# Feed-forward part and output projection of a sequence placed one step later from the first gate product on, in a six-layer windowed-attention network

## Chip, core and metric

The kernel runs on one core of one Trainium2 chip. The metric is the device time in microseconds (us) of one launch of the whole program, the median of three runs. The core has five engines that run beside each other and meet at semaphores: PE (TensorE, matmul), DVE (VectorE), ACT (ScalarE), POOL (GpSimd) and SP (SyncE, which issues the DMAs here). Each engine takes its instructions strictly in the order in which they are written: an instruction that waits holds up everything behind it on its engine.

## The reference, cut to what matters

The program computes two outer levels; nearly 70% of its time goes to a network of six layers on 8 sequences of 512 tokens with 128 features. This is the part that the change touches:

```python
for i in range(DEPTH):                       # DEPTH = 6
    x = attn_layer(shift_tokens(x), Wqkv[i], q_scale[i], k_scale[i], Wo[i]) + x
    x = ffn_layer(shift_tokens(x), ln_g[i], ln_b[i], W1[i], b1[i], W2[i], b2[i]) + x

def attn_layer(x, Wqkv, qs, ksc, Wo):        # 16 heads of 64
    q, k, v = split(x @ Wqkv)
    q = l2norm(q) * qs;  k = l2norm(k) * ksc
    q, k = rotary(q), rotary(k)
    out = local_attention(q, k, v)           # window 32, looks back one window
    return out @ Wo                          # the output projection

def ffn_layer(x, g, bln, W1, b1, W2, b2):
    xn = (x - x.mean()) / sqrt(var + 1e-05) * g + bln
    a, gate = split(xn @ W1 + b1)            # 341 hidden features each
    return a * gelu(gate) @ W2 + b2
```

## The kernel before, in words

The network lies in the function `network`. Features are on the 128 partitions and the 512 tokens of one sequence on the free axis. A **turn** is one sequence in one layer: 6 x 8 = 48 turns, which the rows number 0 to 47. A turn has 20 **steps** (`NS = STEPS = 20`), numbered n = 0 to 19; a step handles four heads and one of five windows of queries, so n = 5g + t with head group g and window t. Every engine runs the same loop over turns and steps (`turns`), and its own function `step` says in what order it does its share of step n.

In one step the engines pass on this chain. PE computes the scores (`scores`, L491 and L496), DVE takes the row maxima (`row_max`, L706), ACT the exponentials with their sums (`exp`, L385). One step later DVE inverts the sums (`inv_sum`, L715) and POOL scales (`normalise`, L323). Two steps after the scores PE transposes the probabilities (`turn_probs`, L506), DVE copies them out of PSUM (`pt_copy`, L722), PE multiplies by the values (`values`, L520) and ACT copies the result into `OT` (`out_copy`, L396).

Beside that each step does a piece of the projections of later head groups: `proj` (L465 to L467) and `v_proj` (L477 to L479) are three matmuls each into the one-bank PSUM tiles PA or PB; ACT squares them (`square`, L363), DVE multiplies them by the rotary tables (`products`, L685), POOL adds (L329, L335), PE sums the squares (`sumsq`, L472), ACT forms the inverse norm (L368, L370), DVE finishes (`finish`, L696) and SP rearranges the result by DMA. Since PA and PB are single, a projection waits until DVE or ACT has read the one before it. `v_copy` (L701 on DVE, L374 on ACT) takes the values out.

The third strand is the tail of the *previous* sequence (`prev`), spread over the steps of the present one, on the one PSUM bank PC:

- output projection, eight products `out_proj(p)` (L530): p = 0, 1, 2 in steps 17, 18, 19 of its own turn, the rest in steps 0 to 3 of the next;
- `residual` (L731) on DVE in step 4, `centre` (L535) on PE in step 6, `variance` (L539) and `scale` in step 7;
- three gate products `gate(c)` (L548) in steps 8, 9, 11, copied by ACT (L412); in step 11 ACT does the three gelus (L417) with a table load before and one after them (L417, L418);
- three value products `value(c)` (L556) in steps 12, 13, 14, each followed on DVE by `hidden(c)` (L745) at the head of the next step, since all three share the bank PC;
- three products `outer(c)` (L562): 0 and 1 at the end of step 15, 2 ahead of the scores of step 16; `outer(0)` waits for all three `hidden`;
- `finish_turn` (L752) on DVE in step 17, which frees PC and writes the sequence's new state. `out_proj(0)` of the present sequence waits for it.

The order is written out by hand in the `step` functions; no scheduler changes it. A product of 512 columns in fp32 appears in the trace as two MATMUL records of one instruction (L530, L535, L548, L556, L562, L472).

Turns 7, 15, 23, 31, 39 (the last sequence of a layer that has a successor) also carry the loading and splitting of the next layer's weights on DVE (L771, L773, in steps 1, 4, 6, 9, 14, 16) and the making of its tables (steps 11 and 14). Turn 0 has no previous sequence. After turn 47 the same steps are run once more for the tail of the last sequence alone.

## Time and profile before

| what | value |
|---|---|
| median of 3 runs | 6478.83 us (6478.44 to 6481.75) |
| the profiled execution's own time | 6476.3 us |
| its span, first to last instruction | 6474.1 us |
| mean granted TensorE clock | 0.922 |
| busy: PE, DVE, ACT, POOL | 85%, 66%, 58%, 40% |
| first and last row maximum (L706) of the network | at 2027.7 and 6414.5 us |

The profile shows one execution. 4386.8 us lie between the first and the last of the 960 row maxima (one in each step of the 48 turns). Times in the timeline are microseconds from the start of the span. A value in brackets at the end of a timeline row is the time for which the engine stood idle before it, and what ended the idle time. Steps are counted here from one row maximum to the next. The granted clock is a share of TensorE's full rate of 2.4 GHz; it is either 1.00 or 0.50, and values between are means over a stretch.

### The profile page before, as it was taken

The numbers are of one execution on the slowest core, as the hardware profiler recorded it, in microseconds if no ns is written. First come the engines' busy times: TensorE is split into PE (matmuls) and PEld (weight loads), VectorE is DVE, ScalarE is ACT, GpSimd is POOL, SyncE is SP. The second block draws the span as 40 slices with busy tenths as digits, with TensorE's granted clock in tenths as the row PEclk, the third lists the DMA queues.
The fourth block names the chain that finished last, engine by engine and source line by source line (L and its number), as shares of the span: only waits on it lengthen the run. The fifth ranks groups of instructions, "written<-read, shape, count | busy, mean of one in ns | idle before, by whom it ended". The sixth has DMA issues, their size and how long they took to land. (4 is left out here: it accounts for less than half of the span.)

```text
span 6474.1 us, 104407 instructions
## 1 busy us (share of the span) xinstructions
PE 5529.6 (85%) x31008; PEld 3052.4 (47%) x31008; DVE 4304.2 (66%) x6942; ACT 3742.1 (58%) x11798; POOL 2598.5 (40%) x2011
## 2 busy tenths in 40 slices
PE   6777777677777999899998999899998999999997
PEld 2333333222224555555555555555555555555554
DVE  6667666433335777777777777777777677777775
ACT  3344344223224776667676667666776677667775
POOL 1111222000003555455554555455555555555553
PEclk8888888777778999999999999999999999999998
DMA  0000000000002221222222222221222222222222
GB/s 37 0 0 0 0 0 0 20 0 0 0 0 82 47 50 47 53 54 48 49 52 51 51 49 48 53 54 47 48 49 56 51 47 49 56 51 50 47 49 66
DMA packets 160227, 244.42 MB, mean 38 GB/s; under 512 B 51280, under 2 KB 51280, under 8 KB 158928
## 3 DMA queue, kind: packets, MB, share of 16 engines
q1 hardware_dynamic: 159696, 238.08, 15.0%
q8 instruction: 243, 3.98, 0.3%
q14 instruction: 288, 2.36, 0.1%
HBM read 30.26 MB, written 6.29 MB: 6 GB/s over the span
## 5 line engine op out<-in xcount | busy, mean ns | idle before, releaser
L323 POOL TENSOR_TENSOR c_Pb<-c_Pb,c_rs 96x512 f32<-96x512 f32 (+1 forms) x960 | 996.7, 1038 | 1460.4 <-DVE c_rs L715 1460.4
L385 ACT ACTIVATE c_Pb<-c_S,c_nb 96x128 f32<-96x128 f32 (+1 forms) x3840 | 1344.2, 358 | 159.7 <-DVE c_nb L706 158.7
L722 DVE COPY c_PTs<-c_S 128x384 f32<-128x384 f32 (+1 forms) x960 | 558.2, 581 | 627.0 <-PE c_S L506 626.2
L706 DVE TENSOR_REDUCE c_nb<-c_S 96x4 f32<-96x512 f32 (+1 forms) x960 | 657.4, 685 | 403.2 <-PE c_S L496 402.9
L335 POOL TENSOR_TENSOR c_rot<-c_tAB 128x1024 f32<-128x1024 f32 x384 | 911.9, 2375 | 0.8 <-DVE c_tAB L685 0.8
L396 ACT ACTIVATE c_OT<-c_PO 128x192 f32<-128x192 f32 (+1 forms) x960 | 323.6, 337 | 772.9 <-PE c_PO L520 772.0
L385 ACT ACTIVATION_READ_ACCUMULATOR c_Pb<-c_S,c_nb 96x1 f32 (+1 forms) x3840 | 756.5, 197 | 0.0
L329 POOL TENSOR_TENSOR c_sqs<-c_sq 128x512 f32<-128x512 f32 x384 | 487.8, 1270 | 612.6 <-ACT c_sq L363 612.6
L496 PE MATMUL c_S<-c_QK 64*96 64x128 f32 (+1 forms) x7680 | 667.9, 293 | 0.0
L506 PEld LDWEIGHTS c_S<-c,c_Pb 96*128 96x128 f32 (+1 forms) x3840 | 434.8, 142 | 370.2 <-issue 215.6
L520 PE MATMUL c_PO<-c_PTs,c_V 128*64 128x96 f32 (+1 forms) x7680 | 557.6, 267 | 20.2 <-issue 19.2
L496 PEld LDWEIGHTS c_S<-c_QK 64*96 64x96 f32 (+1 forms) x7680 | 464.5, 166 | 185.8 <-issue 185.8
L506 PE MATMUL c_S<-c,c_Pb 96*128 96x96 f32 (+1 forms) x3840 | 508.8, 255 | 10.9 <-issue 10.9
L491 PE MATMUL c_S<-c 128*96 128x256 bf16 (+1 forms) x1920 | 389.1, 285 | 145.2 <-DVE c_PTs L722 128.8
L992 POOL TENSOR_TENSOR a_AT<-a_AT,c 128x256 f32<-128x256 f32 x128 | 112.2, 876 | 906.0 <-ACT a_AT L1050 905.7
L491 PEld LDWEIGHTS c_S<-c 128*96 128x96 bf16 (+1 forms) x1920 | 170.3, 118 | 622.8 <-DVE c_PTs L722 476.8
L520 PEld LDWEIGHTS c_PO<-c_PTs,c_V 128*64 128x64 f32 x7680 | 365.3, 137 | 158.9 <-issue 31.3
L530 PE MATMUL c_PC<-c_OT,c_WT 128*128 128x512 f32 x768 | 413.1, 630 | 0.5 <-issue 0.5
L1135 PE MATMUL a_B<-a_AT,a_V 128*32 128x512 f32 (+3 forms) x1024 | 331.9, 471 | 81.7 <-POOL a_AT L993 81.7
L368 ACT ACTIVATE c_lnr<-c_PA,c 128x512 f32<-128x512 f32 x192 | 132.0, 687 | 286.8 <-PE c_PA L472 286.8
L363 ACT ACTIVATE c_sq<-c_PB 128x512 f32<-128x512 f32 x384 | 229.6, 598 | 113.2 <-PE c_PB L467 106.4
L1407 POOL COPY xf<-b_xn 64x512 f32 x8 | 6.6, 823 | 676.4 <-DVE b_xn L1550 676.4
(264 smaller groups left out, 10945.7 us busy)
## 6 DMA issues: line engine op xcount, KB each, us to landing
c_QK<-c_F SPq DMA_DIRECT2D x3072, 64.0 KB, 2.0
c_stage<-in_w_heads SPq DMA_DIRECT2D x36, 256.0 KB, 2.9
c_WT<-in_w_tails SPq DMA_DIRECT2D x6, 537.5 KB, 4.9
b_W<-in_w_level SPq DMA_DIRECT2D x1, 3133.0 KB, 10.3
a_W<-in_w_level SPq DMA_DIRECT2D x1, 3078.0 KB, 10.3
c_WT<-in_w_tails SPq DMA_DIRECT2D x6, 512.0 KB, 3.7
x<-in_x SPq DMA_DIRECT2D x1, 2048.0 KB, 7.4
x_kept<-x SPq DMA_DIRECT2D x1, 2048.0 KB, 6.3
```

The costliest lines, as they stand in the source:

```text
L323: nc.gpsimd.tensor_tensor(p, p, r, ALU.mult).then_inc(*p_ready.up())
L329: nc.gpsimd.tensor_tensor(sqs[:, :], sq[:, 0], sq[:, 1], ALU.add).then_inc(*added.up())
L335: nc.gpsimd.tensor_tensor(rot[:, :, :], tAB[:, 0], tAB[:, 1], ALU.add).then_inc(*rotated.up())
L385: e = nc.scalar.activation(Pb[0:m, n % 3, i, :], S[0:m, 2 * (n % 2) + r, c * SPAN_K:(c + 1) * SPAN_K], ACT.Exp, bias=nb[0:m, n % 2, i:i + ...
L491: nc.tensor.matmul(S[0:m, 2 * (n % 2) + r, 0:2 * SPAN_K], const.identb[:, 0:m], const.mask[t > 0], start=True, stop=False, skip_group_chec ...
L496: mm = nc.tensor.matmul(S[0:m, 2 * (n % 2) + r, c * SPAN_K:(c + 1) * SPAN_K], QK[rows, g % 2, 0, c, q0:q0 + m], QK[rows, g % 2, 1, c, k0:k ...
L506: mm = nc.tensor.transpose(S[:, 2 * (n % 2) + r, to:to + m], Pb[0:m, n % 3, 2 * r + c, :], ident[0:m, 0:m])
L520: mm = nc.tensor.matmul(PO[64 * r:64 * r + 64, c * TILE:c * TILE + m], V[:, t, h * DH:(h + 1) * DH], PTs[:, n % 2, 2 * r + c, 0:m], start= ...
L530: nc.tensor.matmul(PC[:, :], WT[:, T_O + p * P:T_O + (p + 1) * P], OT[:, p, :], start=p == 0, stop=p == PAIRS - 1, skip_group_check=True). ...
L706: nc.vector.tensor_reduce(nb[0:m, n % 2].rearrange("p (b c) -> p b c", b=2), S[0:m, b:b + 2, 0:2 * SPAN_K].rearrange("p b (c k) -> p b c k ...
L722: nc.vector.tensor_copy(PTs[:, n % 2].rearrange("p (b c) q -> p b c q", b=2)[:, :, :, 0:m], S[:, b:b + 2, 2 * SPAN_K:].rearrange("p b (c q ...
L1135: mm = nc.tensor.matmul(B[32 * j:32 * j + 32, 6 + g % 2, i * TILE:SEQ], V[:, i, h, :], AT[:, h % 2, SPAN[i]:SPAN[i] + SEQ - i * TILE], sta ...
```

## The change

It changes on which step each part of the tail lies, and for some parts the place inside the step. No instruction is added or taken away inside the 48 turns; the run for the tail after turn 47 has 20 steps in place of 18.

| part | before | after |
|---|---|---|
| `out_proj` p = 0, 1 of the present sequence | steps 17, 18 | steps 18, 19 |
| `out_proj` p = 2 | step 19 | step 0 |
| p = 3, 4, 5 of the previous | steps 0, 1, 2 | p = 3 in step 1, 4 in step 2, 5 in step 3 |
| p = 6, 7 | both in step 3 | step 3 and step 4 |
| `residual` | step 4 | step 5 |
| `value(1)`, `value(2)` | steps 13, 14 | steps 14, 15 |
| `hidden(0)` | step 13, ahead of `inv_sum` | step 13, behind the last `products` |
| `hidden(1)`, `hidden(2)` | steps 14, 15 | steps 15, 16 |
| `outer(0)`, `outer(1)` | end of step 15 | 0 ahead of the scores of step 16, 1 at its end |
| `outer(2)` | step 16, ahead of the scores | end of step 16 |
| `finish_turn` | step 17 | step 18 |

So step 17 has one product of `out_proj` fewer and step 4 one more; `centre`, `variance`, `scale`, the gates, the gelus and `value(0)` stay where they were.

```diff
             l = depth - 1
...
-            for n in range(18):
+            for n in range(NS):
                 step(n, None, None, at(l, seqs - 1), None, False)
...
                     if n == 1 and prev:
-                        out_proj(4, prev, None)
+                        out_proj(3, prev, None)
...
                     if n == 16 and prev:
-                        outer(2, prev)
+                        outer(0, prev)
...
-                    if now and n in (17, 18, 19):
-                        out_proj(n - 17, now, prev)
+                    if now and n in (18, 19):
+                        out_proj(n - 18, now, prev)
                     if prev:
-                        for p in {0: (3,), 2: (5,), 3: (6, 7)}.get(n, ()):
+                        for p in {0: (2,), 2: (4,), 3: (5, 6), 4: (7,)}.get(n, ()):
                             out_proj(p, prev, None)
                         if n in (8, 9):
                             gate(n - 8, prev)
-                        if n in (12, 13, 14):
-                            value(n - 12, prev)
-                        if n == 15:
-                            outer(0, prev)
+                        for c in {12: (0,), 14: (1,), 15: (2,)}.get(n, ()):
+                            value(c, prev)
+                        if n == 16:
                             outer(1, prev)
+                            outer(2, prev)
...
-                    if prev and n in (13, 14, 15):
-                        hidden(n - 13, prev)
+                    if prev and n in (15, 16):
+                        hidden(n - 14, prev)
                     if t1:
                         inv_sum(m1, t1)
...
-                        if n == 4:
+                        if n == 5:
                             residual(prev)
-                        if n == 17:
+                        if n == 18:
                             finish_turn(prev)
...
                     if t == 3 and tq:
                         products(jq, 1, tq)
+                    if prev and n == 13:
+                        hidden(0, prev)
```

Three places show what an engine finds in its queue. First PE in step 16, from the transposes of step 14's probabilities (L506) on. L491 and L496 are the scores, L520 the values, L472 the sum of squares, L562 an `outer` product. Before:

```order
L506 MATMUL c_S<-c,c_Pb 128x96 [waits c_p_ready]
L506 MATMUL c_S<-c,c_Pb 128x96 x3
L562 MATMUL c_PC<-c_hh,c_WT 128x512
L491 MATMUL c_S<-c 96x256 [waits c_pt_copied]
L491 MATMUL c_S<-c 96x256
L496 MATMUL c_S<-c_QK 96x128 x4
L520 MATMUL c_PO<-c_PTs,c_V 64x96 [waits c_v_dve1,c_po_copied,c_pt_copied]
L520 MATMUL c_PO<-c_PTs,c_V 64x96 x3
L470 REGISTER_ALU
L471 REGISTER_ALU [waits c_added]
L472 MATMUL c_PB<-c_sqs,c 128x512 [waits c_prods]
```

Now:

```order
L506 MATMUL c_S<-c,c_Pb 128x96 [waits c_p_ready]
L506 MATMUL c_S<-c,c_Pb 128x96 x3
L562 MATMUL c_PC<-c_hh,c_WT 128x512 [waits c_h_ready]
L491 MATMUL c_S<-c 96x256 [waits c_pt_copied]
L491 MATMUL c_S<-c 96x256
L496 MATMUL c_S<-c_QK 96x128 x4
L520 MATMUL c_PO<-c_PTs,c_V 64x96 [waits c_v_dve1,c_po_copied,c_pt_copied]
L520 MATMUL c_PO<-c_PTs,c_V 64x96 x3
L470 REGISTER_ALU
L471 REGISTER_ALU [waits c_added]
L472 MATMUL c_PB<-c_sqs,c 128x512 [waits c_prods]
L562 MATMUL c_PC<-c_hh,c_WT 128x512 x2
```

The `outer` product ahead of the scores is now the one that waits for `c_h_ready`, the signal of `hidden`, and two more follow at the step's end; before, the one ahead of the scores had no wait of its own.

Second, DVE in steps 17 and 18. L722 is `pt_copy`, L715 `inv_sum`, L752 `finish_turn` (two halves of the partitions), L701 `v_copy`, L706 the row maximum, L696 `finish`. Before:

```order
L722 COPY c_PTs<-c_S 128x512 [waits c_pv_done,c_pt_done]
L715 RECIPROCAL c_rs<-c_sums 96x4 [waits c_p_ready,c_exps]
L752 SCALAR_TENSOR_TENSOR xf<-c_PC,c_WT,c_x1s 64x512 [waits c_w2_done]
L752 SCALAR_TENSOR_TENSOR xf<-c_PC,c_WT,c_x1s 64x512
L700 REGISTER_ALU
L701 COPY c_V<-c_PA 128x512 [waits c_v_done0]
L705 REGISTER_ALU
L706 TENSOR_REDUCE c_nb<-c_S 96x4 [waits c_s_done]
L689 REGISTER_ALU
L696 SCALAR_TENSOR_TENSOR c_F<-c_PB,c_rot 128x1024 [waits c_perm7,c_rinvs,c_rotated]
L722 COPY c_PTs<-c_S 128x4x96 [waits c_pv_done,c_pt_done]
L715 RECIPROCAL c_rs<-c_sums 96x4 [waits c_p_ready,c_exps]
```

Now:

```order
L722 COPY c_PTs<-c_S 128x512 [waits c_pv_done,c_pt_done]
L715 RECIPROCAL c_rs<-c_sums 96x4 [waits c_p_ready,c_exps]
L700 REGISTER_ALU
L701 COPY c_V<-c_PA 128x512 [waits c_v_done0]
L705 REGISTER_ALU
L706 TENSOR_REDUCE c_nb<-c_S 96x4 [waits c_s_done]
L689 REGISTER_ALU
L696 SCALAR_TENSOR_TENSOR c_F<-c_PB,c_rot 128x1024 [waits c_perm7,c_rinvs,c_rotated]
L722 COPY c_PTs<-c_S 128x4x96 [waits c_pv_done,c_pt_done]
L715 RECIPROCAL c_rs<-c_sums 96x4 [waits c_p_ready,c_exps]
L752 SCALAR_TENSOR_TENSOR xf<-c_PC,c_WT,c_x1s 64x512 [waits c_w2_done]
L752 SCALAR_TENSOR_TENSOR xf<-c_PC,c_WT,c_x1s 64x512
```

`finish_turn` has left the place ahead of `v_copy` in step 17 and stands in step 18 ahead of the `products` (L685) and the row maximum that follow there.

Third, DVE in steps 4 and 5, where L731 is `residual`. Before:

```order
L715 RECIPROCAL c_rs<-c_sums 96x4 [waits c_p_ready,c_exps]
L731 TENSOR_TENSOR c_x1s<-c_PC,xf 64x512 [waits c_wo_done]
L731 TENSOR_TENSOR c_x1s<-c_PC,xf 64x512
L705 REGISTER_ALU
L706 TENSOR_REDUCE c_nb<-c_S 96x4 [waits c_s_done]
L701 COPY c_V<-c_PB 128x512 [waits c_v_done1]
L722 COPY c_PTs<-c_S 128x4x96 [waits c_pv_done,c_pt_done]
L715 RECIPROCAL c_rs<-c_sums 96x4 [waits c_p_ready,c_exps]
L689 REGISTER_ALU
L696 SCALAR_TENSOR_TENSOR c_F<-c_PA,c_rot 128x1024 [waits c_perm2,c_rinvs,c_rotated]
```

Now:

```order
L715 RECIPROCAL c_rs<-c_sums 96x4 [waits c_p_ready,c_exps]
L705 REGISTER_ALU
L706 TENSOR_REDUCE c_nb<-c_S 96x4 [waits c_s_done]
L701 COPY c_V<-c_PB 128x512 [waits c_v_done1]
L722 COPY c_PTs<-c_S 128x4x96 [waits c_pv_done,c_pt_done]
L715 RECIPROCAL c_rs<-c_sums 96x4 [waits c_p_ready,c_exps]
L731 TENSOR_TENSOR c_x1s<-c_PC,xf 64x512 [waits c_wo_done]
L731 TENSOR_TENSOR c_x1s<-c_PC,xf 64x512
L689 REGISTER_ALU
L696 SCALAR_TENSOR_TENSOR c_F<-c_PA,c_rot 128x1024 [waits c_perm2,c_rinvs,c_rotated]
```

`residual` has moved from the place ahead of step 4's row maximum to the place ahead of `finish` (L696) and of step 5's row maximum.

## Rows read from the trace of the kernel before

**Rows 1.** Page, part 1: busy time, share of span, instructions.

```profile
PE 5529.6 (85%) x31008; PEld 3052.4 (47%) x31008; DVE 4304.2 (66%) x6942; ACT 3742.1 (58%) x11798; POOL 2598.5 (40%) x2011
```

**Rows 2.** Windows: turns 18, 19 and 23; last columns clock, DMA share, GB/s.

```profile
3679.90:3769.10 89.20, 83.09 (x574) 49.95 (x576) 64.97 (x103) 63.24 (x226) 48.96 (x36) 1.00 0.21 48
...
3769.10:3858.80 89.70, 84.10 (x574) 51.15 (x576) 65.13 (x103) 63.25 (x226) 48.95 (x36) 0.98 0.21 48
...
4128.40:4237.10 108.70, 92.30 (x574) 55.83 (x576) 83.95 (x124) 63.59 (x226) 50.04 (x36) 0.91 0.20 47
```

**Rows 3.** Timeline, turn 18 step 12 and 13: start, duration, engine, line.

```profile
3733.30 1.28 ACT L418 ACT_TABLE_LOAD   x1
...
3733.48 0.74 DVE L745 SCALAR_TENSOR_TENSOR c_hh<-c_PC,c_WT,c_hh 128x512 f32<-128x512 f32 x1
...
3735.56 1.12 PE L556 MATMUL c_PC<-c_xn,c_WT 128*128 128x512 f32 x2
...
3736.39 0.17 DVE L715 RECIPROCAL c_rs<-c_sums 96x4 f32<-96x4 f32 x1 [2.16 <-ACT c_Pb L385]
...
3736.87 1.23 DVE L685 TENSOR_TENSOR c_tAB<-c_PA,c_TA 128x1024 f32<-128x1024 f32 x1 [0.31 <-ACT c_sq L363]
...
3738.15 0.50 PE L477 MATMUL c_PA<-c_WH,c_xh 128*128 128x512 f32 x1 [1.47 <-DVE c_tAB L685]
```

**Rows 4.** Timeline, turn 18 from the end of step 15 through step 16.

```profile
3746.80 1.98 PE L562 MATMUL c_PC<-c_hh,c_WT 128*128 128x512 f32 x4
...
3749.30 0.49 PE L506 MATMUL c_S<-c,c_Pb 96*128 96x96 f32 x4
...
3749.63 1.05 PE L562 MATMUL c_PC<-c_hh,c_WT 85*128 85x512 f32 x2
...
3749.83 0.56 DVE L722 COPY c_PTs<-c_S 128x384 f32<-128x384 f32 x1 [0.96 <-PE c_S L506]
...
3750.52 0.38 PE L491 MATMUL c_S<-c 128*96 128x256 bf16 x2
...
3752.89 0.60 PE L506 MATMUL c_S<-c,c_Pb 128*128 128x128 f32 x4
```

**Rows 5.** Timeline, turn 18 steps 17 to 19.

```profile
3754.22 1.50 DVE L752 SCALAR_TENSOR_TENSOR xf<-c_PC,c_WT,c_x1s 64x512 f32<-64x512 f32 x2
...
3754.27 0.42 PE L491 MATMUL c_S<-c 128*96 128x256 bf16 x2
...
3755.75 0.69 DVE L701 COPY c_V<-c_PA 128x512 f32<-128x512 f32 x1
...
3756.36 0.68 DVE L706 TENSOR_REDUCE c_nb<-c_S 96x4 f32<-96x512 f32 x1
...
3756.50 0.50 PE L465 MATMUL c_PA<-c_xh,c_WH 128*128 128x512 f32 x1 [0.61 <-DVE c_V L701]
...
3757.29 1.02 PE L530 MATMUL c_PC<-c_OT,c_WT 128*128 128x512 f32 x2
...
3759.24 1.19 DVE L685 TENSOR_TENSOR c_tAB<-c_PA,c_TA 128x1024 f32<-128x1024 f32 x1
...
3762.59 0.60 ACT L374 ACTIVATE c_V<-c_PA 128x512 f32<-128x512 f32 x1
...
3762.67 0.47 PE L477 MATMUL c_PB<-c_WH,c_xh 128*128 128x512 f32 x1
```

**Rows 6.** Timeline, turn 18 steps 4 and 5.

```profile
3695.64 1.38 DVE L731 TENSOR_TENSOR c_x1s<-c_PC,xf 64x512 f32<-64x512 f32 x2
...
3698.85 0.50 PE L465 MATMUL c_PB<-c_xh,c_WH 128*128 128x512 f32 x1 [0.43 <-DVE c_V L701]
...
3699.95 1.23 DVE L696 SCALAR_TENSOR_TENSOR c_F<-c_PA,c_rot 128x1024 f32<-128x1024 f32 x1
...
3701.23 0.50 PE L465 MATMUL c_PA<-c_xh,c_WH 128*128 128x512 f32 x1
```

**Rows 7.** Windows: turn 19 after the wait in step 13.

```profile
3827.20:3830.60 3.40, 3.25 (x10) 2.66 (x11) 2.74 (x5) 1.97 (x9) 0.91 (x1) 0.50 0.01 3
```

## The prediction

> **What bounds the kernel now.** I read the page first, then the windows by turn, then the timeline of one turn, and in it only the bracketed waits of PE and what ended them. The page [rows 1] shows the busy shares of the whole program; the windows of single turns say more [rows 2]. An ordinary turn (18) takes 89.2 us, in which PE has matmuls under way for 83.1, DVE for 65.0, ACT for 63.2 and POOL for 49.0. So PE stands still for only 6.1 us of a turn, and the three others are there to keep it fed. The change takes no matmul away, so in the 48 turns it can win at most those 6.1 us, and it loses whatever new waits it gives PE. The question is thus which PE waits go and which come, step by step. I replay the moved pieces on turn 18, whose clock stayed at 1.00, with each piece's duration and its distance to the next taken from the rows. All times are those of the timeline before, and "late" is against it.
>
> What the reader should see first is the longest hole, in step 13 [rows 3]. PE finishes `value(1)` (L556 from 3735.56) and waits 1.47 us, until 3738.15, for the `products` (L685) that free PA. These stand on DVE behind `inv_sum` (L715), which waited 2.16 us for ACT's exponentials; ACT was late since its gelus and the table load behind them (L418) end at 3734.58.
>
> **Step 13: the hole stays, and loses its filling.** The end of the hole hangs on ACT alone, and nothing on ACT moves. `hidden(0)` (L745, 3733.48 to 3734.22) leaves its place ahead of `inv_sum`, but `inv_sum` waited another 2.16 us after it, so that is worth nothing [rows 3]. `value(1)`, which PE did inside the hole for free, leaves it. `hidden(0)` now runs behind the second `products`, over a microsecond before `value(1)` wants it at the end of step 14; it pushes `pt_copy` back by its 0.7 us, where the scores of step 14 still have more than that to spare. In steps 14 and 15 a value product takes the place of a later one. Price so far: nothing on the clock, but one product now has to be paid elsewhere.
>
> **Steps 15 and 16: a saving, then a wait and two products.** An fp32 product costs PE 0.86 us when it stands behind another (four matmuls 1.98, two 1.12 [rows 3, 4]). Step 15 has one product where it had two: 0.86 early, so `turn_probs` (L506) starts at 3748.44 in place of 3749.30. Its copy L722 follows 0.53 behind [rows 4], at 3748.97. Then comes `hidden(2)`, 0.47 later and 0.74 long: it ends at 3750.18. `outer(0)`, now ahead of the scores, waits for it until 3750.23, though PE is free at 3748.77 (0.33 behind L506, as in [rows 4]). That is a new wait of 1.46 us. The scores follow 0.89 behind, at 3751.12: 0.60 late. Queued behind the waiting product are just these scores, and so the row maximum, the exponentials and all of step 16. At the step's end come `outer(1)` and `outer(2)`, 2 x 0.86 = 1.72. PE enters step 17 2.32 us late.
>
> **Step 17: part of it comes back.** `finish_turn` (L752, 1.50 us) no longer stands ahead of `v_copy` (L701), so PE's 0.61 us wait for it goes [rows 5]; with rounding 0.68. `out_proj(0)` (L530) goes too, 0.86. Late by 0.78. But without that product PE is at step 18's projection before DVE has finished: the row maximum can only start 1.08 behind the late scores, at 3757.67, and `finish` follows it for 1.2. That is a wait of some 0.35. Late by 1.13.
>
> **Steps 18 and 19: `finish_turn` where it is in the way.** It now stands ahead of the `products` (L685, 3759.24 before [rows 5]). `inv_sum` before it waits for the late exponentials until about 3760.06, then 1.53 for `finish_turn`: `products` start at 3761.68, the row maximum at 3762.81, the second `products` end at 3764.63, all 2.44 late. PE needs these to reuse PA and PB: `v_proj` on PB (L477, 3762.67 before) starts at 3764.68, 2.0 late. The next matmul waits for ACT's `v_copy` (L374, 3762.59 before), which stands behind exponentials that are 2.44 late; that makes it 2.3. What DVE gained in step 17 is no use here, since its chain restarts at the late exponentials. Term 1: **2.3 us a turn**. Bounds: 1.1 if PE could pass steps 18 and 19 without the DVE wait, 2.44 if it follows ACT in full.
>
> **Steps 4 and 5: the same with `residual`.** Before, L731 (1.38 us) lay in step 4, in a stretch where DVE idled for the scores anyway. `out_proj(7)` now stands at the end of step 4: 0.86, of which PE's 0.43 wait for L701 [rows 6] is eaten. This alone would be at least 0.3 late. Then `residual` delays L696 from 3699.95 to 3701.32, and PE's projection onto PA (L465, 3701.23) waits for L696: it starts at 3702.60. The row maximum of step 5, the exponentials and the squares behind it are late by the same 1.37. No engine has slack left in step 6: PE's sum of squares there already waited for POOL and ACT. The product and the delay overlap, so term 2 is **1.37 us a turn**; bounds 0.4 (the product alone) and 1.8 (both in a row).
>
> **Sum.** Ordinary turns, of which there are 41: 2.3 + 1.37 = 3.67, in all 150 us. The five turns that carry the next layer's weights (turn 23: 108.7 us [rows 2]) are bound by DVE's splitting in steps 14 to 17; there the `outer` products fall into PE's idle time and DVE's sum is unchanged, so only term 2 counts: 7 us. Turn 47 lacks the next sequence's projections: 2 us. Turn 0 moves one product: nothing. In the extra run after turn 47 the tail is one chain in which each piece waits for the one before, in the same order; the two further steps hold no other work: nothing. That makes 159 us.
>
> **The clock.** In turn 19 the granted clock was 0.50, that is 1.2 GHz, for 3.4 us right after the 1.47 us wait of step 13 [rows 7], and the turn took 89.7 us instead of 89.2; turn 20's fall cost more. In turn 18 the same wait left it at 1.00 [rows 2]. The hole now grows from 1.47 to 2.4 us, and a second of 1.46 appears in step 16. I take it that a fall comes in most turns, and costs 0.5 us a turn more than now on the mean: 20 us. Bounds: 0, and 85 us (two falls in every ordinary turn). The Trainium skill (TensorE: Matmul & The Clock Gate, Part 1: The HAM clock gate) says that half rate is the default and activity releases it; the trace agrees as far as a slow stretch follows the idle one. It speaks against this change, since it makes holes dearer than their length.
>
> So 6476.3 + 159 + 20 = 6655 us for a profiled execution. The one shown ran 2.5 us under the median of the runs, so about **6658 us**, 2.8% slower.
>
> **Rivals.**
> *Only one place costs.* One of the two terms is absorbed: by term 2 alone 46 x 1.37 = 63 us, by term 1 alone 41 x 2.3 + 2 = 96 us, with some clock 6540 to 6590 us. For it: a replay may miss a slack. Against: in both places the delay goes through row maximum and exponentials, the chain that feeds PE. Chance 0.14.
> *The clock decides.* Two or more slow stretches in every turn, 6700 to 6740 us. For it: rows 7. Against: turn 18 took the same wait with none. Chance 0.09.
> *No change.* The Trainium skill (Perfetto Trace Analysis, Identifying the Most-Contended Engine) says matmul busy time misjudges how near TensorE is to its limit and counts weight loads instead. In turn 18 these are busy 50.0 of 89.2 us, DVE is busiest with 65.0, and every engine has over a quarter free [rows 2]. Moved work would then drown in idle time, and the time stays within 13 us of 6479. Against: PE's matmuls follow each other without a gap outside 6.1 us. Chance 0.03.
> *Faster.* The mechanism is in step 13: if `hidden(0)`, which waits for the gelus ahead of `inv_sum`, were what holds DVE, its move would give 0.74 us a turn, and with step 17's 0.61 wait 1.35 x 47 = 63 us: 6415 us. It decides only if the exponentials of step 12 ended by 3734.2; they ended about 3736.35. Chance 0.04.
> My forecast has the remaining 0.70.
>
> **Numbers.** The forecast's own range is 6620 to 6700. The range for 8 in 10 goes to 6570 below, into the first rival, and to 6715 above, into the second. A measurement of this kernel tells apart about 0.2%, 13 us. Faster 0.04, same 0.03, slower 0.93.
>
> **What would show it.** Right: ordinary turns of about 93 us, PE busy time unchanged; in step 13 a PE wait of 2.4 us before L477; in step 16 a PE wait of about 1.4 us before `outer(0)`, ended by `hidden(2)`; no wait for L701 in step 17; waits before both L477 in steps 18 and 19, ended by `products`; in step 5 about 1 us before the projection onto PA, ended by `finish`; more windows at 0.50. Wrong: the step 16 wait missing or under 0.5 us, step 5 as long as before, or the loop from step 19 to step 4 shorter than before. Turns under 91 us would make the prediction wrong, and so would turns above 95.

## The result and the profile after

The changed kernel takes **6662.59 us** (median of 4 runs, 6659.62 to 6673.99), the kernel before 6478.64 in the same comparison (6478.02 to 6481.75): a ratio of **1.0286, with a 95% interval of 1.0268 to 1.0304**. It is slower, by 184 us; 6658 was forecast. The profiled execution's span is 6661.8 us against 6474.1, so 187.7 us are to be accounted for.

The first row is part 1 of the page after: busy time, share of the span and instructions of each engine.

```profile
PE 5594.5 (84%) x31008; PEld 3089.4 (46%) x31008; DVE 4306.9 (65%) x6942; ACT 3732.8 (56%) x11798; POOL 2600.7 (39%) x2011
```

Against [rows 1] no engine has a different number of instructions, and DVE, ACT and POOL are busy as before. PE is busy 64.9 us longer with the same matmuls, so some of them ran slower: over the span the granted clock was at 0.50 for 1124.9 us where it was for 1008.6 before, and 116.3 us more at half rate account for some 58 us of busy time (an estimate from these two figures). The rest of the 187.7 us, 122.8, is time in which PE stood still. The waits of PE say where. The rows are the engine, the tile and line that waited, what it waited for, and the total in us, the number of times and the longest. After:

```profile
PE c_PA L477 <- DVE c_tAB L685: 105.8, 43, 2.5
...
PE c_PC L562 <- DVE c_hh L745: 62.2, 48, 1.3
...
PE c_PA L465 <- DVE c_F L696: 54.5, 48, 1.9
...
PE c_PB L477 <- DVE c_tAB L685: 28.6, 68, 1.2
...
PE c_PB L465 <- DVE c_V L701: 1.3, 3, 0.4
...
PE c_PA L465 <- DVE c_V L701: 0.8, 1, 0.8
```

And the same view of the kernel before:

```profile
PE c_PA L477 <- DVE c_tAB L685: 65.7, 45, 1.6
...
PE c_PA L465 <- DVE c_V L701: 28.2, 46, 0.8
...
PE c_PB L465 <- DVE c_V L701: 21.3, 50, 0.4
...
PE c_PB L477 <- DVE c_tAB L685: 16.5, 37, 1.2
...
PE c_PA L465 <- DVE c_F L696: 2.1, 1, 2.1
```

Three new waits have come, one in each place the prediction named: for `hidden` before `outer` (62.2 us, 1.3 in each turn), for `finish` before the projection onto PA (54.5 for 2.1), and 40.1 us more in the hole of step 13. The two waits for `v_copy` went, but for 0.8 of 28.2 and 1.3 of 21.3. The wait for `products` before the L477 onto PB grew by 12.1; it is that of step 18, below.

Windows of the changed kernel, turns 18, 19, 20, 21 and 23; columns are length, then busy time and instructions of PE, PEld, DVE, ACT and POOL, then granted clock, DMA share and GB/s:

```profile
3740.50:3835.40 94.90, 86.17 (x574) 51.95 (x576) 65.13 (x103) 63.09 (x226) 48.98 (x36) 0.96 0.19 46
3835.40:3929.20 93.80, 84.95 (x576) 51.47 (x578) 65.14 (x104) 63.00 (x226) 48.98 (x36) 0.98 0.20 46
3929.20:4023.40 94.20, 85.06 (x574) 50.79 (x574) 64.95 (x102) 63.09 (x226) 48.98 (x36) 0.98 0.20 46
4023.40:4116.90 93.50, 84.80 (x574) 51.43 (x576) 65.18 (x104) 63.01 (x226) 48.98 (x36) 0.98 0.20 46
4211.20:4315.00 103.80, 88.00 (x574) 53.35 (x575) 82.80 (x123) 63.40 (x226) 49.82 (x36) 0.95 0.20 49
```

An ordinary turn is one of the 41 that have a previous sequence, carry no weights and are not the last. Turn 18, 89.2 us at clock 1.00 in [rows 2], is 94.9 at 0.96; no ordinary turn keeps a clock of 1.00 any more. On the mean an ordinary turn took 89.98 us before and takes 94.54 now. Turn 23, which carries weights, went the other way, from 108.7 to 103.8 us at a clock of 0.95 instead of 0.91.

The single places in turn 21, PE only. Steps 13 to 16:

```profile
4079.97 0.55 PE L520 MATMUL c_PO<-c_PTs,c_V 128*64 128x96 f32 x8 [0.43 <-issue]
4083.05 0.80 PE L477 MATMUL c_PA<-c_WH,c_xh 128*128 128x512 f32 x1 [2.52 <-DVE c_tAB L685]
...
4084.49 0.84 PE L506 MATMUL c_S<-c,c_Pb 96*128 96x96 f32 x4
...
4088.63 1.13 PE L556 MATMUL c_PC<-c_xn,c_WT 128*128 128x512 f32 x2
...
4093.80 0.49 PE L506 MATMUL c_S<-c,c_Pb 96*128 96x96 f32 x4
4095.60 1.13 PE L562 MATMUL c_PC<-c_hh,c_WT 128*128 128x512 f32 x2 [1.30 <-DVE c_hh L745]
4096.57 0.38 PE L491 MATMUL c_S<-c 128*96 128x256 bf16 x2
...
4098.93 1.88 PE L562 MATMUL c_PC<-c_hh,c_WT 128*128 128x512 f32 x4
```

Without `value(1)` in it the hole is 2.52 us long where it was 1.47 [rows 3], and the L477 behind it takes 0.80 instead of 0.50, in a stretch at half rate. The window over that stretch reads

```profile
4082.84:4086.25 3.41, 3.20 (x10) 2.63 (x11) 3.17 (x6) 1.97 (x9) 1.12 (x2) 0.50 0.04 10
```

`outer(0)` waits 1.30 us for `hidden(2)`, with the scores (L491) queued behind it, and the other two (1.88 us) stand at the end of the step. Steps 5, 17 and 18 on PE, and `finish_turn` on DVE:

```profile
4046.11 0.50 PE L465 MATMUL c_PA<-c_xh,c_WH 128*128 128x512 f32 x1 [1.12 <-DVE c_F L696]
...
4103.58 0.50 PE L465 MATMUL c_PA<-c_xh,c_WH 128*128 128x512 f32 x1
...
4107.19 1.12 PE L530 MATMUL c_PC<-c_OT,c_WT 128*128 128x512 f32 x2
...
4110.13 0.50 PE L477 MATMUL c_PB<-c_WH,c_xh 128*128 128x512 f32 x1 [0.42 <-DVE c_tAB L685]
```

```profile
4105.59 1.50 DVE L752 SCALAR_TENSOR_TENSOR xf<-c_PC,c_WT,c_x1s 64x512 f32<-64x512 f32 x2
4107.12 1.22 DVE L685 TENSOR_TENSOR c_tAB<-c_PA,c_TA 128x1024 f32<-128x1024 f32 x1
```

The wait of 0.61 in step 17 [rows 5] is gone, 1.12 stand before the projection that was without a wait in step 5 [rows 6], and `products` now follow `finish_turn`, with 0.42 of wait before the L477 on PB.

Row maximum to row maximum over the whole loop, by kind of turn and by step, the difference is made up like this (a delay in front of the row maximum of step n shows in the length of step n - 1):

| part | us |
|---|---|
| 41 ordinary turns x 4.55 | +186.7 |
| in them: step 4 | +1.40 a turn |
| step 13 (clock) | +0.80 |
| steps 14, 15, 16 | +0.04, +0.65, +0.71 |
| steps 17, 18 | +1.14, -0.15 |
| step 0 | -0.04 |
| five weight turns | -9.7 |
| turn 47 | +9.8 |
| tail run | +2.0 |
| before the loop, turn 0 | -1.2 |

### The profile page after: what moved, and what is told of

Read it like the earlier page. It is cut to its first block and busy times, and to the rows that moved or that the text cites. A ratio compares the mean times of both kernels' runs of the same rounds, so it can differ in the third digit from the quotient of the medians.

```text
span 6661.8 us, 104407 instructions
## 1 busy us (share of the span) xinstructions
PE 5594.5 (84%) x31008; PEld 3089.4 (46%) x31008; DVE 4306.9 (65%) x6942; ACT 3732.8 (56%) x11798; POOL 2600.7 (39%) x2011
## 5 line engine op out<-in xcount | busy, mean ns | idle before, releaser
L706 DVE TENSOR_REDUCE c_nb<-c_S 96x4 f32<-96x512 f32 (+1 forms) x960 | 657.5, 685 | 593.5 <-PE c_S L496 593.0
L722 DVE COPY c_PTs<-c_S 128x384 f32<-128x384 f32 (+1 forms) x960 | 558.4, 582 | 614.3 <-PE c_S L506 610.5
L496 PE MATMUL c_S<-c_QK 64*96 64x128 f32 (+1 forms) x7680 | 668.3, 293 | 0.0
L506 PEld LDWEIGHTS c_S<-c,c_Pb 96*128 96x128 f32 (+1 forms) x3840 | 445.3, 144 | 373.4 <-issue 233.4
L520 PE MATMUL c_PO<-c_PTs,c_V 128*64 128x96 f32 (+1 forms) x7680 | 555.2, 266 | 20.0 <-issue 19.3
L496 PEld LDWEIGHTS c_S<-c_QK 64*96 64x96 f32 (+1 forms) x7680 | 465.1, 166 | 187.6 <-issue 187.6
L506 PE MATMUL c_S<-c,c_Pb 96*128 96x96 f32 (+1 forms) x3840 | 514.2, 257 | 12.8 <-issue 11.1
L491 PE MATMUL c_S<-c 128*96 128x256 bf16 (+1 forms) x1920 | 390.8, 286 | 137.2 <-DVE c_PTs L722 120.0
L491 PEld LDWEIGHTS c_S<-c 128*96 128x96 bf16 (+1 forms) x1920 | 178.8, 119 | 618.3 <-DVE c_PTs L722 440.1
L520 PEld LDWEIGHTS c_PO<-c_PTs,c_V 128*64 128x64 f32 x7680 | 363.7, 137 | 158.4 <-issue 30.1
L465 PE MATMUL c_PA<-c_xh,c_WH 128*128 128x512 f32 x384 | 225.5, 587 | 83.3 <-DVE c_F L696 54.5
## 6 DMA issues: line engine op xcount, KB each, us to landing
b_W<-in_w_level SPq DMA_DIRECT2D x1, 3133.0 KB, 10.3
```

The costliest lines, as they stand in the source:

```text
L491: nc.tensor.matmul(S[0:m, 2 * (n % 2) + r, 0:2 * SPAN_K], const.identb[:, 0:m], const.mask[t > 0], start=True, stop=False, skip_group_chec ...
L496: mm = nc.tensor.matmul(S[0:m, 2 * (n % 2) + r, c * SPAN_K:(c + 1) * SPAN_K], QK[rows, g % 2, 0, c, q0:q0 + m], QK[rows, g % 2, 1, c, k0:k ...
L506: mm = nc.tensor.transpose(S[:, 2 * (n % 2) + r, to:to + m], Pb[0:m, n % 3, 2 * r + c, :], ident[0:m, 0:m])
L520: mm = nc.tensor.matmul(PO[64 * r:64 * r + 64, c * TILE:c * TILE + m], V[:, t, h * DH:(h + 1) * DH], PTs[:, n % 2, 2 * r + c, 0:m], start= ...
L706: nc.vector.tensor_reduce(nb[0:m, n % 2].rearrange("p (b c) -> p b c", b=2), S[0:m, b:b + 2, 0:2 * SPAN_K].rearrange("p b (c k) -> p b c k ...
L722: nc.vector.tensor_copy(PTs[:, n % 2].rearrange("p (b c) q -> p b c q", b=2)[:, :, :, 0:m], S[:, b:b + 2, 2 * SPAN_K:].rearrange("p b (c q ...
```

## The experiments

Ten kernels were run. Each ratio is against the kernel before in the same comparison. Its median was 6475.44 us for the first four kernels, 6480.48 for the two without the gelu, the one with `value(0)` in the hole and the first tuned version, and 6476.04 for the one with all `outer` products at the end and the second tuned version.

**`residual` alone.**

```diff
-                        if n == 4:
+                        if n == 5:
                             residual(prev)
```

> The kernel before, with nothing changed but `residual`, which goes from step 4 to step 5. The theory (a piece costs what the chain behind it has no slack for): `finish` and the row maximum of step 5 come 1.38 us late, PE's projection onto PA with them, in 47 turns: 6479 + 47 x 1.38 = about 6543 us; step 4 as long as before (3.58 us), step 5 1.4 longer (5.3). The rival (the longer step 4 comes from its additional product of the output projection, and `residual` is hidden wherever it stands): no change, 6470 to 6490 us.

Measured: 6539.6 us, 1.0093 (1.0076 to 1.011). Moving one DVE instruction pair of 1.38 us, which DVE has ample time for, costs 64 us: 1.33 in step 4 of each ordinary turn (1.22 over the whole turn, 50.0 in all, where the clock falls in 15 of them and in 22 before), 9.4 us in the five weight turns, 5.6 in turn 47. That DVE is idle for a third of the span was no protection. DVE and then PE in turn 19:

```profile
3811.45 1.38 DVE L731 TENSOR_TENSOR c_x1s<-c_PC,xf 64x512 f32<-64x512 f32 x2
3812.86 1.23 DVE L696 SCALAR_TENSOR_TENSOR c_F<-c_PA,c_rot 128x1024 f32<-128x1024 f32 x1
```

```profile
3814.14 0.50 PE L465 MATMUL c_PA<-c_xh,c_WH 128*128 128x512 f32 x1 [1.37 <-DVE c_F L696]
```

The wait is as long as the instruction that was put ahead of `finish`. The rival that foresees no change is out. I had expected the delay in the length of step 5; it delays the row maximum of step 5, and so counts to step 4.

**The feed-forward part alone** (values, hiddens and outers moved; output projection, `residual` and `finish_turn` as before).

```diff
                     if n == 16 and prev:
-                        outer(2, prev)
+                        outer(0, prev)
...
-                        if n in (12, 13, 14):
-                            value(n - 12, prev)
-                        if n == 15:
-                            outer(0, prev)
-                            outer(1, prev)
+                        for c in {12: (0,), 14: (1,), 15: (2,)}.get(n, ()):
+                            value(c, prev)
+                        if n == 16:
+                            outer(1, prev)
+                            outer(2, prev)
...
+                    if prev and n == 13:
+                        hidden(0, prev)
...
-                    if prev and n in (13, 14, 15):
-                        hidden(n - 13, prev)
+                    if prev and n in (15, 16):
+                        hidden(n - 14, prev)
```

> The kernel before, with only the value products, `hidden` and the `outer` products moved as in the change; output projection, `residual` and `finish_turn` as before. The theory: the whole loss of steps 13 to 19 comes from these: about 2.3 us a turn in steps 15 to 17, and 0.8 us in step 13 from a clock that now falls in every turn: 41 x 3.1 = 127 us, about 8 more in the last turn: 6600 to 6620 us. Step 4 stays at 3.58 us, the wait for `v_copy` in step 17 stays. The rival (`finish_turn` in step 18, ahead of `products`, is what costs in steps 17 to 19): only the wait for `hidden(2)` counts, 0.6 us a turn and the clock, 6530 to 6545 us.

Measured: 6585.94 us, 1.0171 (1.0154 to 1.0188). The mechanism held and the time lies below the expected 6600 to 6620, far above the rival's 6530 to 6545: steps 14 to 16 cost 2.40 a turn (2.3 expected), the clock in step 13 only 0.35 where 0.8 was assumed, and the weight turns gained 10.3 us. The wait that makes it, in turn 19, is the same as in the changed kernel:

```profile
3878.43 1.12 PE L562 MATMUL c_PC<-c_hh,c_WT 128*128 128x512 f32 x2 [1.30 <-DVE c_hh L745]
```

**Output projection, `residual` and `finish_turn` alone** (feed-forward part as before).

```diff
-            for n in range(18):
+            for n in range(NS):
                 step(n, None, None, at(l, seqs - 1), None, False)
...
                     if n == 1 and prev:
-                        out_proj(4, prev, None)
+                        out_proj(3, prev, None)
...
-                    if now and n in (17, 18, 19):
-                        out_proj(n - 17, now, prev)
+                    if now and n in (18, 19):
+                        out_proj(n - 18, now, prev)
...
-                        for p in {0: (3,), 2: (5,), 3: (6, 7)}.get(n, ()):
+                        for p in {0: (2,), 2: (4,), 3: (5, 6), 4: (7,)}.get(n, ()):
...
-                        if n == 4:
+                        if n == 5:
                             residual(prev)
-                        if n == 17:
+                        if n == 18:
                             finish_turn(prev)
```

> The kernel before, with only the output projection, `residual` and `finish_turn` moved as in the change; value products, `hidden` and `outer` as before. The theory: step 4 or 5 together 1.4 us longer; in steps 17 to 19 the 1.5 us that PE gains in step 17 (wait for `v_copy`, one product) are lost again to `finish_turn` in step 18, net 0.1 us; the clock falls no more often than before: 6479 + 47 x 1.5 = about 6545 us (6535 to 6560). The rival (`finish_turn` costs): 1.5 us a turn more, 6600 to 6620 us.

Measured: 6547.5 us, 1.0107 (1.0091 to 1.0124), inside the first range. Step 4 costs 1.40 a turn. The rest comes to nothing: step 16 is 1.01 shorter, step 17 is 1.14 longer, step 18 0.15 shorter, together -0.02. The 0.42 that PE waits before `v_proj` on PB is there:

```profile
3877.55 0.50 PE L477 MATMUL c_PB<-c_WH,c_xh 128*128 128x512 f32 x1 [0.42 <-DVE c_tAB L685]
```

but the product of 0.86 that left step 17 and the wait for `v_copy` pay for it. So what `finish_turn` costs in step 18 is just what its leaving and the product's win before it, and the rival, by which it costs 1.5 us a turn more, is out. Of the changed kernel's steps 14 to 18 the feed-forward part makes 2.40 and this part nothing.

**The changed kernel with the step 3 and 4 of before.**

```diff
-                        for p in {0: (2,), 2: (4,), 3: (5, 6), 4: (7,)}.get(n, ()):
+                        for p in {0: (2,), 2: (4,), 3: (5, 6, 7)}.get(n, ()):
...
-                        if n == 5:
+                        if n == 4:
                             residual(prev)
```

> The changed kernel, with `out_proj(7)` back in step 3 (which then has three products) and `residual` back in step 4; all else as in the change. The theory: step 4 falls from 4.97 to 3.58 us, step 3 grows by one product, 0.86: 0.53 us a turn less than the change, 6662 - 47 x 0.53 = about 6637 us. PE's wait of 1.12 us for `finish` in step 5 goes, the one of 0.43 us for `v_copy` in step 4 comes back. The rival (the eighth product costs, not `residual`): the product costs as much in step 3 as in step 4, so 6655 to 6665 us.

Measured: 6637.25 us, 1.0249 (1.0232 to 1.0266). Against the changed kernel step 3 gets 0.86 longer by its third product and step 4 1.40 shorter. The product has to be paid in either place; what `residual` costs over it is 0.54 a turn.

**The gelus taken out of the kernel before.** ACT does an identity with the bias in place of the three gelus, and both table loads go; the output lacks the gelu.

```diff
-                        nc.scalar.activation(hh[0:m, c], hh[0:m, c], ACT.Gelu, ...)
-                    nc.scalar.preload_act_table_set("natural_log_exp_and_others")
+                        nc.scalar.activation(hh[0:m, c], hh[0:m, c], ACT.Identity, ...)
```

> The kernel before without the gelu: ACT adds the bias only (Identity), and so needs no table load in step 11 and none behind it. This leaves out the gelu of the feed-forward part. The theory: ACT comes 2 x 1.28 = 2.56 us earlier out of step 11, the hole of step 13 closes but for PE's own work (value(1) takes half a microsecond of it), 2.05 us a turn and the falls of the clock (0.35): 6475 - 47 x 2.4 = about 6362 us (6350 to 6380).

Measured: 6345.15 us, 0.9793. A little below the range: the hole and its clock cost 3.05 a turn (step 12 2.68, step 13 0.37), and the waits of steps 12 and 13 are gone.

**The same in the changed kernel**, again without the gelu.

> The changed kernel without the gelu and its two table loads, as in the kernel beside it. The theory: the loss in steps 4 and 14 to 18 has nothing to do with the hole and stays (1.40 + 2.39 us a turn), the clock no longer falls in step 13 (0.8), and with no hole to lose, leaving out value(1) there wins about 0.5: the distance to the kernel before without gelu is 41 x 3.3 = 135, less 10 in the turns with weights, plus 8 in the last: 125 to 140 us instead of 184. The rival (the hole of step 13 is what the moved work misses; without it the same work costs the same wherever it stands): a distance of 60 us or less, the 1.4 of step 4.

Measured: 6504.22 us, 1.0042; its difference from the kernel above is 152.2 us in the spans and 159 in the medians, where 125 to 140 were expected. The rival, under which the change costs at most 60 us without the hole, is out; the expectation was too low, for a part since I credited `value(1)` with 0.5 a turn and it brought 0.12. The rows show the hole closed, at a line number one lower, in turn 19:

```profile
3832.69 0.50 PE L476 MATMUL c_PA<-c_WH,c_xh 128*128 128x512 f32 x1 [0.21 <-DVE c_tAB L684]
```

Steps 4, 14, 15, 16, 17 and 18 differ by 1.40, 0.04, 0.64, 0.71, 1.15 and -0.13, to 0.02 the same as with the gelus. Step 13 no longer differs, and no ordinary turn has a fall of the clock there. So the 0.80 of step 13 belongs to the hole, and the other terms don't depend on it.

**The changed kernel with `value(0)` in the hole**, in step 13 in place of 12.

```diff
-                        for c in {12: (0,), 14: (1,), 15: (2,)}.get(n, ()):
+                        for c in {13: (0,), 14: (1,), 15: (2,)}.get(n, ()):
```

> The changed kernel with value(0) moved from the end of step 12 to the end of step 13, into the hole. PE's idle time in steps 12 and 13 is as long as in the change, but it lies in two pieces, about 1.3 us ahead of the values and 1.6 us behind the product. One theory (the clock falls because of the 2.5 us hole in one piece): it falls less often, and up to 0.8 us a turn come back: 6630 to 6645 us. The other (only the sum of idle time about step 13 counts): the clock falls in every ordinary turn as before, 6655 to 6668 us.

Measured: 6650.66 us, 1.0265 (1.0248 to 1.0282), between the two ranges. PE stands still 1.06 us before the product and 1.47 behind it:

```profile
3893.19 0.55 PE L520 MATMUL c_PO<-c_PTs,c_V 128*64 128x96 f32 x8 [1.06 <-issue]
3893.67 1.13 PE L556 MATMUL c_PC<-c_xn,c_WT 128*128 128x512 f32 x2
3896.27 0.50 PE L477 MATMUL c_PA<-c_WH,c_xh 128*128 128x512 f32 x1 [1.47 <-DVE c_tAB L685]
```

The clock still falls in 37 of 41 ordinary turns, against 17 in the kernel before with its single wait of 1.47, and 41 in the changed kernel; step 13 is 0.25 shorter on the mean. It settles neither theory: two waits of 1.06 and 1.47 make the clock fall nearly as often as the 2.52 of the changed kernel, which has 0.43 before its values, and cost a little less.

**The changed kernel with all three outer products at the end of step 16.**

```diff
-                    if n == 16 and prev:
-                        outer(0, prev)
...
                         if n == 16:
+                            outer(0, prev)
                             outer(1, prev)
                             outer(2, prev)
```

> The changed kernel, with outer(0) taken from ahead of the scores of step 16 to the end of that step, ahead of outer(1) and outer(2). Theory (half of what steps 15 and 16 cost is the wait of the scores behind outer(0), half the second product that comes into step 16): the scores of step 16 start right behind pt_copy, 1.6 us earlier in the turn than in the changed kernel, the 1.30 us wait for hidden(2) goes, and the third product costs its 0.86 at the step's end. Net 0.75 us a turn, 41 x 0.75 = 31 us: 6625 to 6640 us, steps 15 and 16 together 9.9 us in place of 10.7. Rival (the row maximum of step 16 stands on DVE behind products and cannot start more than 0.9 us earlier, so exponentials and squares hold PE before the products): under 0.3 us a turn, 6650 to 6662 us.

Measured: 6646.85 us, 1.0266 (1.0252 to 1.028), between the ranges, with the rival's mechanism. PE and DVE in turn 21 (line numbers are one lower on DVE):

```profile
4087.43 0.42 PE L491 MATMUL c_S<-c 128*96 128x256 bf16 x2 [0.65 <-DVE c_PTs L721]
...
4089.18 1.12 PE L472 MATMUL c_PB<-c_sqs,c 128*128 128x512 f32 x2 [0.24 <-POOL c_sqs L329]
4090.14 2.74 PE L562 MATMUL c_PC<-c_hh,c_WT 128*128 128x512 f32 x6
```

```profile
4088.03 1.19 DVE L684 TENSOR_TENSOR c_tAB<-c_PA,c_TB 128x1024 f32<-128x1024 f32 x1
4089.14 0.68 DVE L705 TENSOR_REDUCE c_nb<-c_S 96x4 f32<-96x512 f32 x1
```

The row maximum starts directly behind `products`, 0.94 earlier and not 1.6, and PE waits 0.65 and 0.24 in new places. Step 15 is 0.94 shorter, step 16 0.52 longer: 0.42 a turn, of which falls of the clock take some back (an ordinary turn as a whole is 0.26 shorter). A wait of 1.30 us taken away is thus worth 0.42; 0.89 of it PE would have waited anyway.

**The kernel before, tuned by its own small waits.** In the first version `v_copy` stands ahead of the row maximum in steps 4, 9, 14 and 19, and ahead of `finish_turn` in step 17:

```diff
                     if t == 3 and tq:
                         products(jq, 0, tq)
+                    if t == 4 and tq:
+                        v_copy(*{4: (1, 1), 9: (1, 3), 14: (0, 1), 19: (0, 4)}[n], PB, tq)
                     if now:
                         row_max(n, now)
```

> The kernel before with two pieces of DVE's order changed: in steps 4, 9, 14 and 19 `v_copy` stands ahead of the row maximum, for which DVE idles 0.5 to 1.8 us there, and in step 17 `v_copy` stands ahead of `finish_turn`. What the experiments so far say: a wait of PE that goes is worth something only if the row maximum does not come later and no other wait takes over. In step 9 PE's wait of 0.59 us for `pt_copy` goes, worth 0.5; in step 4 the wait of 0.43 goes but the row maximum comes 0.2 late, worth 0.1 to 0.2; in step 17 0.61 go and `finish` takes over but for 0.1. Together 0.6 to 0.8 us a turn: 6440 to 6450 us. The rival (PE waits simply add up, so all three are won): 1.6 us a turn, 6400 us.

Measured: 6470.64 us, 0.9987 (0.9977 to 0.9997); both theories were wrong. In step 4 PE's 0.43 wait went and 0.78 came in its place:

```profile
3787.73 0.50 PE L465 MATMUL c_PA<-c_xh,c_WH 128*128 128x512 f32 x1 [0.78 <-DVE c_F L696]
```

In step 9 `v_copy` ran earlier and the wait of 0.59 stayed, because the copy behind it on DVE took twice as long (below, on the hardware). Of the three places only step 17 gained, 0.15 a turn, and step 3 got 0.16 longer. The second version keeps that edit alone:

```diff
-                        if n == 17:
-                            finish_turn(prev)
...
                         v_copy(0, 2, PA, nxt)
+                    if n == 17 and prev:
+                        finish_turn(prev)
```

> The kernel before with finish_turn in step 17 behind v_copy in place of ahead of it, and nothing else. Theory (PE's 0.61 us wait for v_copy becomes one of 0.41 for finish, as in the kernel that also moved v_copy ahead of the row maxima): 0.15 us a turn, 6 us, 6465 to 6476 us, ratio 0.998 to 1.000. Rival (that kernel's gain lay in the weight turns, by v_copy's place in steps 4, 9, 14 and 19): the time of before within 3 us.

Measured: **6458.84 us, 0.9974 (0.9962 to 0.9986)**, the fastest kernel here that computes the whole function. It lies below both ranges: 6465 to 6476 was expected, and the rival's was the time of before within 3 us. Its step 17 is 0.15 shorter again, with PE waiting 0.40 for `finish` where it waited 0.61 for `v_copy`; In all 11.1 us come in the ordinary turns, 2.7 in the weight turns. Only 6 us of that are step 17; step 13, which the edit does not touch, is 0.06 a turn shorter with a fall of the clock in 14 turns and not in 17, and no run shows whether the edit brings that. So the mechanism is shown for a gain of 6 us, and the rest isn't explained.

## Why the prediction came out right, point by point

The forecast lay 5 us under the measured time, and most of its terms held one by one; a part of the closeness is luck: the clock and turn 47 were forecast too low, the weight turns too high, and these misses cancel.

*Steps 13 to 18, forecast 2.3 a turn: 2.39.* The places were right. The wait for `hidden(2)` shows as 1.30 us of idle time; counted as the forecast did, from where `outer(0)` would have started, 0.33 behind the L506 at 4093.80, to its start at 4095.60, it is 1.47 (forecast 1.46). The row maximum of step 17 is 1.40 late beside the clock, and PE's projection, which followed it by 0.14 before and by 0.47 now, 1.73: forecast were 1.64 (2.32 less 0.68). The row maximum of step 18 is 2.54 late (forecast 2.44), and the turn leaves step 18 with 2.39. The wait for `finish` in step 17 shows as some 0.1 us of idle time, but L465 starts 0.59 behind the L506 at 4104.40 where it was 0.28 in turn 18 before (3758.15 and 3758.43): a delay of 0.31 for the 0.35 forecast. Before and after, on PE:

```profile
3758.15 0.49 PE L506 MATMUL c_S<-c,c_Pb 96*128 96x96 f32 x4
3758.43 0.48 PE L465 MATMUL c_PB<-c_xh,c_WH 128*128 128x512 f32 x1
```

```profile
4104.40 0.49 PE L506 MATMUL c_S<-c,c_Pb 96*128 96x96 f32 x4
4104.99 0.50 PE L465 MATMUL c_PB<-c_xh,c_WH 128*128 128x512 f32 x1
```

In the first pair L465 starts 0.21 ahead of the end of the L506 records, so the idle time that a row shows is less than the delay. That `finish_turn` takes back in step 18 what its leave gave before it is what the second half by itself shows: -1.01, then +0.99.

*Steps 4 and 5, forecast 1.37: 1.40.* With `residual` alone 1.33, with the product too 1.40: the two overlap, as forecast.

*The clock, forecast 0.5 a turn: 0.80.* A fall came in every ordinary turn (41; before 17). This is the term that was sized too low. Step 13 lasts 4.7 to 5.1 us without a fall and 5.3 to 6.9 with one, and three groups show. Where the stretch at 0.50 is 3.41 us long and begins at most 0.6 us behind the row maximum of step 13, the step takes 5.3 to 5.6; the 0.43 us that PE otherwise waits before the L477 onto PB is gone in these turns, so the slow matmuls take up a wait that was there anyway. Where it begins 1.6 to 2.4 us behind, that wait stays and the step takes 6.1 to 6.3. And in 13 turns of the changed kernel the stretch is twice as long and the step takes 6.5 to 6.9, as in turn 18:

```profile
3799.54:3806.34 6.80, 6.20 (x18) 3.99 (x20) 3.57 (x6) 2.77 (x11) 4.51 (x4) 0.50 0.05 12
```

In the kernel before all 17 stretches in step 13 are short. With the feed-forward part alone all 41 turns have a fall too, but only one is long, and step 13 costs 0.35. The Trainium skill (TensorE: Matmul & The Clock Gate, Part 1: The HAM clock gate) says that half rate is the default and activity releases it; the runs agree so far that without the hole no ordinary turn has a fall in step 13.

*Weight turns, forecast +7: -9.7.* Here the step failed that said "only term 2 counts". The output projection's half did cost 6.8 us, but the feed-forward half, put at nothing, won 10.3. (Together these make -3.5; the other 6.2 us of the -9.7 no run explains.) Over the five turns the time at a clock of 0.50 fell from 99.0 to 68.3 us, which at half rate is up to 15 us of work. In the five kernels with gelus and the feed-forward part in its old place this time is 88.7 to 105.8 us, in the five with it moved 47.8 to 78.5, so the gain goes with that part. Which of its moves brings it was not tried by a run of its own; the 47.8 is with all three `outer` products at the end of step 16, and there the five turns are another 10.4 us shorter.

*Turn 47, forecast +2: +9.8.* Windows of its steps 14 to 16, before and then after:

```profile
6395.91:6407.76 11.85, 9.96 (x82) 5.79 (x82) 6.27 (x13) 5.59 (x28) 3.83 (x4) 1.00 0.00 0
```

```profile
6574.01:6592.91 18.90, 16.16 (x78) 8.65 (x80) 5.43 (x12) 5.14 (x27) 3.05 (x3) 0.62 0.00 0
```

PE's busy time went from 9.96 to 16.16 us at a mean clock of 0.62, with one value product more in it (0.86 at full rate). The three steps are 7.05 us longer, and the clock was at 0.50 from 6567.7 to 6588.2, where the kernel before has none of that in them. The replay counted waits at full rate, so its 2 us had no term for it.

*The tail run, forecast nothing: +2.0.* `out_proj(2)` comes one step later there too, so `residual` starts 9.45 us after the last row maximum and not 8.59.

*The sum.* Ordinary turns without the clock 154 for 150, clock in them 33 for 20, all else +0.9 for +9: 187.7 for 179. One sign of being right failed beside the sum: "PE busy time unchanged" was forecast and it grew by 64.9 us, as the forecast's own clock term should have said.

*The rivals.* "Only one place costs" is out: each half alone costs about its own term (1.0171 and 1.0107, together 1.028). "Faster", by the leave of `hidden(0)`, is out: `inv_sum` waits 2.83 us for the exponentials in the trace after where it waited 2.16 behind `hidden(0)`. "No change", which reads the headroom from busy shares, is out by the 1.0286. "The clock decides" holds for a sixth of the loss in the ordinary turns.

## What to carry to other kernels

Where one engine is fed by a chain of others with single buffers, price a moved instruction by what stands directly behind it in its own queue and who waits for that: 1.38 us on an engine that idled a third of the time cost 1.33 us in step 4 of every ordinary turn. A wait taken out is worth only as much as the next limit lies behind it (1.30 us of wait was worth 0.42, 0.61 worth 0.15), so look at the next one before counting the gain. And a hole that was filled by work from elsewhere should not be emptied, since the tensor engine's clock may add its own price behind it (here 0.35 and 0.80 us a turn).

## What the runs showed of the hardware

**DVE and POOL get in each other's way, by the operands.** In the first version above, step 9 of turn 19:

```profile
3804.16 2.35 POOL L335 TENSOR_TENSOR c_rot<-c_tAB 128x1024 f32<-128x1024 f32 x1
...
3805.53 1.27 DVE L675 CAST c_xh<-xf 128x512 fp32r<-128x512 f32 x1
```

POOL's add ends at 3806.51, the copy at 3806.80. Started later, at 0.67 us length, it ended just as late. In all 46 cases of before and all 47 of this version in which L675 started under a POOL add, it ended 0.28 to 0.29 us after that add; alone, in the three other cases, it takes 0.41 to 0.43. The subtraction L773, with two inputs in SBUF, takes 0.69 alone (21 of 36) and 2.72 to 2.75 when it starts under a POOL add (15), ending 0.55 behind it. In turn 23 of before it met one:

```profile
4216.84 2.55 POOL L335 TENSOR_TENSOR c_rot<-c_tAB 128x1024 f32<-128x1024 f32 x1
...
4217.19 2.75 DVE L773 TENSOR_TENSOR c_WL<-c_stage,c_WH 128x512 fp32r<-128x512 f32 x1
```

Both end 0.14 sooner behind the add than their lone length would say. So such a DVE instruction does all but some 0.14 us of its work only when POOL's has ended, and what its length in the trace exceeds the lone one by is waiting. DVE instructions with an input in PSUM (L685, L696, L701, L722) run beside POOL at their usual length. The Trainium skill (SBUF — State Buffer, Who interferes with whom) describes this as a port pair that the two share and that one of them holds for a whole instruction; these numbers agree.

**The price of a fall of the clock depends on its length and on where it lands.** In step 13 the clock stays at 0.50 for 3.41 us, as in [rows 7], or for 6.83, and the step gets 0.4 to 1.4 us longer with the first and 1.6 to 2.0 with the second. A single turn's price is therefore no good estimate for the mean.
